# Graph attention on Trainium2: three of a chunk's four gathers take 128 rows instead of two

## The reference

```python
src, dst = edge_index                       # 200000 edges, dst sorted
xw = (x @ W).reshape(N, H, C)               # N = 6250, H = 8, C = 32
a_src = einsum('nhc,hc->nh', xw, att_src)
a_dst = einsum('nhc,hc->nh', xw, att_dst)
e = leaky_relu(a_src[src] + a_dst[dst], 0.2)
alpha = softmax of e over the edges of one dst
out = segment_sum(xw[src] * alpha, dst)     # then + bias, relu
```

## Time and profile before

| | before |
|---|---|
| time, median of 3 runs | 3235.82 us (3235.3 to 3238.56) |
| the profiled execution's own time | 3240.07 us |
| its span, first to last instruction | 3238.3 us |
| mean granted TensorE clock | 0.904 |
| PE, PEld, DVE, ACT, POOL busy | 81%, 53%, 67%, 45%, 64% of the span |
| indirect gathers of `node_rows` | 1616, 976 ns each in the mean |

### The profile page before, as it was taken

The page is one execution under the profiler, slowest core; times in us unless marked ns, Lnnn a source line. Parts: engine busy times, 40 slices in busy tenths (PEclk is TensorE's granted clock), DMA queues, the critical chain, the costliest instruction groups (busy, mean ns, idle before and its releaser), DMA issues. The chain is left out here.

```text
span 3238.3 us, 54302 instructions
## 1 busy us (share of the span) xinstructions
PE 2620.3 (81%) x12344; PEld 1709.4 (53%) x12344; DVE 2165.1 (67%) x5140; ACT 1459.4 (45%) x3473; POOL 2079.2 (64%) x2145
## 2 busy tenths in 40 slices
PE   2999978888887888888787888888755438999996
PEld 1455444444544455454444454554444437888884
DVE  5888877767777676777777676777767844333335
ACT  1444465545555555555464555555433221222226
POOL 0577777777777777777777777777775572222224
PEclk9999989989999898999899989889986559999998
DMA  5222244444545444454444444444443156777867
GB/s 146 44 46 45 41 141 136 141 137 130 142 130 142 131 139 134 136 142 130 142 131 136 136 136 136 136 134 132 134 132 90 58 183 188 232 233 233 233 203 244
DMA packets 303697, 454.51 MB, mean 140 GB/s; under 512 B 121983, under 2 KB 198072, under 8 KB 303442
## 3 DMA queue, kind: packets, MB, share of 16 engines
q0 software_dynamic: 88848, 243.01, 26.7%
q1 hardware_dynamic: 186434, 135.90, 15.7%
q10 hardware_dynamic: 28176, 72.95, 6.9%
HBM read 396.32 MB, written 56.94 MB: 140 GB/s over the span
## 5 line engine op out<-in xcount | busy, mean ns | idle before, releaser
L219 POOL DMA_INDIRECT rows_g<-node_rows,idx x1616 | 1577.9, 976 | 497.8 <-issue 461.1
L1211 PE MATMUL p_m<-msg,sel 128*128 128x264 f32 x3616 | 1043.6, 438 | 254.3 <-DVE msg L1179 207.7
L1211 PEld LDWEIGHTS p_m<-msg,sel 128*128 128x128 f32 x3616 | 727.3, 212 | 390.6 <-issue 272.0
L1179 DVE TENSOR_TENSOR msg<-rows_g,p_w 128x1024 f32<-128x1024 f32 x452 | 550.6, 1218 | 44.8 <-ACT p_w L1077 43.7
L1077 ACT ACTIVATE p_w<-lg 128x32 f32<-128x32 f32 x452 | 91.0, 201 | 785.1 <-DVE lg L1172 783.8
L1863 POOL DMA_INDIRECT moe<-ysb,token x128 | 124.0, 969 | 366.3 <-DVE ysb L1852 343.3
L1168 DVE TENSOR_TENSOR lg<-rows_g,ends 128x32 f32<-128x32 f32 x452 | 87.2, 193 | 406.7 <-SPq L1011 306.0
L1032 ACT ACTIVATE sel_t<-apart,ones 128x512 bf16<-128x512 bf16 x455 | 328.4, 722 | 32.1 <-issue 0.7
L1101 DVE TENSOR_TENSOR sel<-p_w,dst_t 128x512 f32<-128x512 f32 x453 | 312.1, 689 | 26.4 <-issue 9.3
L1029 ACT ACTIVATE apart<-dst_all,iota_neg 128x512 bf16<-128x512 bf16 x455 | 321.6, 707 | 0.0
L1201 PEld LDWEIGHTS p_sp<-adm_parts,sel_t 128*128 128x128 bf16 x1816 | 94.5, 99 | 382.1 <-issue 374.2
(11 more groups left out here) (331 smaller groups left out, 3358.1 us busy)
## 6 DMA issues: line engine op xcount, KB each, us to landing
dst_all<-dst_bc ACTq DMA_DIRECT2D x115, 512.0 KB, 4.2
wa<-in_L_ffn_w_dram SPq DMA_DIRECT2D x64, 512.0 KB, 4.8
wb<-in_L_ffn_w_dram SPq DMA_DIRECT2D x64, 512.0 KB, 5.3
rows_g<-node_rows,idx POOLq DMA_INDIRECT x1616
xs<-slot_x SPq DMA_DIRECT2D x64, 258.0 KB, 2.9
ya<-moe SPq DMA_DIRECT2D x48, 256.0 KB, 4.4
bb<-in_L_ffn_b_dram SPq DMA_DIRECT2D x64, 128.0 KB, 5.6
qs<-xn_turned ACTq DMA_DIRECT2D x13, 512.0 KB
```

What stands on the lines that cost most here:

```text
L219: pool.indirect_dma_start(rows_g[0:n, j, u, :], None, node_rows, bass.IndirectOffsetOnAxis(ap=idx[q][0:n, j, u:u + 1], axis=0)).then_inc(g ...
L1179: dve.tensor_tensor(m4, g3[:, :, 0:D].rearrange("p u (h e) -> p u h e", h=H), p_w[:, 0:TC * H].rearrange("p (u h) -> p u h", u=TC).unsquee ...
L1211: mm = pe.matmul(p_m[j % 2][:, 0:ROW], sel[j][:, u, :], msg[j % 2][:, u, :], start=(u == 0), stop=(u == TC - 1))
```

## The change

`FULL_TILES` goes from 2 to 3. With `CHUNK = 480 + 8 * FULL_TILES` a chunk has 504 edges instead of 496. So `FILLED` goes from 404 to 397 and `STEPS` from 452 to 445. The order of a chunk's gathers becomes one of 120 rows and then three of 128. `CHUNKS`, to which lists are padded, goes from 408 to 400.

```diff
-FULL_TILES = 2
+FULL_TILES = 3
 EXTRA = P - LANES
 BASE = TILES_PER_CHUNK * LANES
 CHUNK = BASE + FULL_TILES * EXTRA
 FILLED = -(-E // CHUNK)
-CHUNKS = 408
+CHUNKS = 400
...
-            for u in (2, 0, 3, 1):
+            for u in (3, 0, 1, 2):
                 n = P if u < FULL_TILES else LANES
                 pool.indirect_dma_start(rows_g[0:n, j, u, :], None, node_rows,
                                         bass.IndirectOffsetOnAxis(ap=idx[q][0:n, j, u:u + 1], axis=0)).then_inc(gathered[j], 16)
```

## The result

The changed kernel takes 3157.43 us (median of 4 runs, 3155.72 to 3159.03) against 3235.61 us of the kernel before (4 runs): ratio 0.9756, 95% interval 0.9744 to 0.9767. That is 78.2 us less, where 74.6 were predicted (3161 us, range 3153 to 3181). The profiled execution took 3159.03 us with a span of 3157.3 us, 81.0 us under the span of before. That is more than 78.2 because the profiled execution of before lay 4.5 us above its median and the one of after only 1.6.

A forecast was written before the change was run, and what follows sets the result against it. The prediction took GpSimd's back-to-back gathers to bound the edge loop, the longest stage. From a median of 3235.82 us it took 74.6 off, 51.6 in the loop and 23.0 in the setup, giving 3161 us, range 3153 to 3181.

The forecast's parts named there:

- What sets the pace: Edge loop: GpSimd issues gathers back to back, 1.2805 us each, its 0.3 us pauses being no waits; VectorE has time in hand.
- a sign of being wrong: Edge loop: the prediction is wrong if GpSimd shows waits of more than 0.3 us on VectorE.
- Part 1 and 2: Edge loop: seven fewer chunks (35.9 us) and a cheaper mix of gather rows (15.7 us), together 51.6 us off.
- the mix of rows: Edge loop: one gather of 120 rows per chunk instead of two, 0.040 us less over 393 chunks, 15.7 us off.
- Which of the two is the dear one: Edge loop: the gather of 120 rows takes 0.99 us, that of 128 rows 0.95; the wrong way round, 15.7 us on top.
- the rival that the rows have nothing to do with it: Edge loop: the gather's 0.04 us is not due to its rows, so 3177 us; chance 0.06.
- Part 3: Setup, SP's queue: the list tail at lines 357 and 359 issues faster with 12 chunks than with 19, 23.0 us off.
- the open bound: Setup: no row shows 12 chunks; 23.4 us go if spread as 8 are, 21.6 with the slowest such issue; 23.0 taken.
- Rival 2: Setup: a smaller gain there; chance 0.09, half of it at 3174 us.
- Costed at nothing: Node stage and stages after the loop as long as before; the four chunks at the seam between stages cost nothing.
- The slower rival: Edge loop: gathers of 128 rows stall without a shorter one between them, making the kernel slower; chance 0.02.

The follow-up runs named there:

- The experiment with three gathers: The changed kernel without the fourth gather of a chunk (120 rows, tile 3), its messages made from zeros: 2918.72 us, ratio 0.9016.
- four full gathers: The changed kernel with all four gathers of a chunk at 128 rows (512 edges, 439 steps): 3110.25 us, ratio 0.9610 to the kernel before.
- the order 0 to 3: The changed kernel with a chunk's gathers in order u = 0, 1, 2, 3, the one of 120 rows last: 3161.17 us, ratio 0.9762.
- the two runs that took it away: Kernel before, list tail as 16 and 3 chunks: 3216.56 us; changed kernel, 19 chunks in one transfer again: 4021.29 us on the chip with pauses.
- the setup's part alone: The kernel before with only its list tail written as 16 and 3 chunks: 4037 us on the chip with pauses, 3216.56 us on another.

## Why the prediction held

**What sets the pace** was right. The loop's waits after are those forecast: 0.3 us before a gather, and 279.5 us of VectorE's waits for chunks where about 280 were said. Besides the first wait of 2.9 us, which the kernel before has too, one of 0.9 us on VectorE stands at the loop's start. By its letter that is a sign of being wrong that the prediction named, but it is one gather in 1572. The experiment with three gathers shows it from the other side.

**Part 1 and 2, the loop**: 51.6 us forecast, 57.2 measured. The mechanism was right and the size of a term was off. Seven chunks at the measured 5.123 us are 35.9, as forecast. The rest, the mix of rows, gave 21.3 instead of 15.7. A chunk was to cost 5.082 us; it costs 1.3007 + 1.2604 + 1.2538 + 1.2535 = 5.068, and 0.0137 us over 393 chunks are 5.4 of the 5.6 us that were missed. Half of it lies in "3 x 1.255": in the median a gather of 128 costs 1.257 us behind one of 120 and 1.251 or 1.250 behind one of 128. The other half lies in the outliers: 0.022 us a chunk were kept, and the mean is 0.015 above the medians. That part may be chance, as it was 0.019 before and with four full gathers. No row of before had two gathers of 128 in a row in the loop, and the setup's pair at 1.26 was too coarse to show it. Nor is 1.250 the price of every 128 behind a 128, as with four of them in a row it was 1.254.

**Which of the two is the dear one** was read rightly from the issue order, and the rival that the rows have nothing to do with it has fallen: with other rows in the same place the price changes (112: 0.94 us), with the same rows in another place it stays (the order 0 to 3: 0.99). That 104 and 120 rows are dear and 112 and 128 not was no part of the prediction. The runs show it for these four values only; what about the number of rows does it, and what GpSimd does longer there, they don't.

**Part 3, the setup**: 23.0 us forecast, 21.8 measured. Lines 357 and 359 went from 24.87 to 1.61 us, 23.3, near the 23.4 summed for 12 chunks spread as 8 are. The rest is 1.7 us that SP's queue was later ahead of line 357, mostly in line 345, which the change doesn't touch. The bias landed at 50.9 and not at 49.5 for the same reason. The trickle as its cause is shown by the two runs that took it away (0.64 us at this line) and put it back (23.17 us). That 12 chunks would go as fast as 8 was the open bound. No row showed it, and the 23.0 was the author's estimate, by the likeness of 12 to 8.

The pace of the packets shows it in the changed kernel. With 19 chunks there were 11.7 ns a packet and 12% of the 16 engines' time, which is the packet time of 1.9 engines; with 8 chunks 1.2 us / 844 = 1.4 ns. With 12 chunks 1086 packets, 1046 of them under 512 B, moved from 36.4 to 37.6 at 58% of the engines' time: 1.1 ns each. With 25 chunks it was 2.2 ns at 40%. So the pace doesn't simply fall with the number of chunks, and what about 19 makes it slow no run shows, nor whether it lies in how the number divides. Rival 2 at 3174 us in the chances stands for a setup that gives only 9.8 us, 840 runs at 11.7 ns, if 12 chunks moved at the pace of 19. No run shows this term either; what the runs showed in its place is the 1.1 ns and the 21.8 us.

**Costed at nothing**: the node stage and the seam behind it took 1.0 us more, the stages after the last gather 3.0 us less. Neither was traced further. In the profiled executions of the other kernels on chips without pauses the stretch after the last gather took 755.9 to 761.6 us, so 3.0 us there can be chance. That the total came within 3.6 us of the forecast is in part luck: the loop's term was 5.6 us too small and the setup's 1.2 too large, and the medians lie 2.8 us closer together than the profiled executions.

**The slower rival** (rival 4 of the chances), full gathers that stall when nothing shorter stands between them, has fallen: four in a row, over the whole loop, cost 1.2587 us each in the mean. The longest of them took 1.47 us instead of 0.95, and 21 of 1564 took over 1.1 us, where it was 24 of 1616 before.

## What to carry to other kernels

Look for the engine whose pauses are all of one length and whose instructions follow without a gap: here it set the pace, even though its busy share (76% of this loop) was below another's (82%), and without one of its four gathers the loop fell from 1990.6 to 1747.8 us. When a constant is changed that sizes a loop, work out what else it sizes: here over a quarter of the gain came from a list's tail going from 19 to 12 chunks, which no line of the diff names, and splitting 19 into 16 and 3 alone gave the kernel before 20 us. And a full indirect transfer of 128 rows cost less than one of 120 or 104 (0.95 us against 0.99) and only 0.01 us more than one of 112, so fill it up before looking for a better order.

## What the runs showed that I had not expected

- An indirect gather's price on GpSimd doesn't follow its rows: 112 rows 0.94 us, 128 rows 0.95, 104 and 120 rows 0.99. A little of the dear ones' price falls on the gather behind them (0.95 to 0.97 us with the dear one in last place).
- One chip ran the same kernel before in 4055 us instead of 3236, with all engines but GpSimd standing still together for some us at a time in the edge loop. In one such pause, from 1506.0 to 1511.5 in the trace of the setup's part alone, no engine but GpSimd did anything, while the DMA engines moved 0.62 MB. What causes it stays open.
